# Two-layer graph attention on one core: both normalisations and one bound moved from VectorE to ScalarE, the centring term made by GpSimd, the mixed phase in another order

## Chip, cores, metric

One core of a Trainium2 chip. The metric is the device time of one launch in microseconds (us). The engines are named as in the profile: PE (TensorE matmul), PEld (its weight loads), DVE (VectorE), ACT (ScalarE), POOL (GpSimd), SP (SyncE, which issues the DMAs).

## What is computed

Sixteen graphs of 512 nodes and 256 channels pass two attention layers. Cut to what matters (biases left out):

```python
# layer 0: one head, masked by adj == 0
q, k = x @ Wq, x @ Wk
s = where(adj == 0, -1e18, q @ k.T / 16)
x = layernorm(x + (where(adj == 0, 0, softmax(s)) @ x) @ Wc)
# layer 1: 8 heads of 32 channels, weighted by the clipped adjacency
s = q_h @ k_h.T / sqrt(32) + log(clip(adj, 1e-8))
out = layernorm(x + concat_h(softmax(s) @ v_h) @ Wo)
```

A layer norm is (x - mean) / sqrt(var + 1e-5), then gamma and beta.

## The kernel before

**Phases.** All five engines run the same list of stages, each its own part of every stage, in the order of that list. `run` (line 422) goes through a first phase (front of graph 0), fifteen mixed phases (order `SCHEDULE`, line 73), a last phase (`LAST`) and an end. A mixed phase works on three graphs: the front of graph j (layer 0, then layer 1's q, k, v and the row maxima of head group 0), the back of graph i (row maxima of head group 1, scores, exponentials, masks and sums of layer 1), and the tail of graph t (output projection, second layer norm, store). `follow` (line 430) lets an engine skip stages in which it has no part; so where a stage stands in the list decides what stands in front of it on each engine's own queue.

**Stages of the front.** `split` makes a high and a low part of x transposed (ACT line 810, DVE line 948). `q0` projects (PE line 598, ACT 815, DVE 964). `bias` compares adj with zero (DVE line 977), which `max0` needs. `u` makes x @ Wc rows and one more column (ACT line 826). `max0` bounds each row's scores (PE lines 650 and 652, DVE line 989). `floor` adds a constant to that extra column (DVE line 995), `shift0` takes the smaller of the two bounds (DVE line 1000) and spreads it as a diagonal (ACT line 832), which the last steps of `scores0` add (PE lines 663 to 668); ACT takes the exponential (line 836). `context0` is the weighted sum (PE line 676), with four DVE instructions for each of four row tiles (1021 to 1029). `stats0` aggregates mean and variance (DVE 1036); POOL makes (var + eps) to the power -0.5 in two instructions (lines 1133, 1135); `norm0` is four DVE instructions, one for each row tile (line 1044). `transpose` turns them (PE 685, ACT 867, DVE 958), and `q1`, `k1`, `v` project (PE 598 and 620). `max1` is one matmul (line 698) and one maximum over 512 columns (DVE line 1005), sixteen in a group of heads; `mrow1` transposes the maxima (PE 703, DVE 1011), and a DMA puts them into the stack that `scores1` reads.

**Stages of the back and the tail.** `scores1` (quad, pair) is two matmuls (line 719), two exponentials (ACT 847) and one mask multiplication on POOL (line 1144), or on DVE where the list has a `mask` stage (line 985). `values1` and `denominators1` sum a quad (PE line 742). The exponentials of quad n wait for both sums of quad n-3. `sums_out` copies both accumulators out (ACT 856, 857), and `values1` and `denominators1` of quad 4 wait for it. `reciprocal` (four parts, DVE 1052), `normalise` (1057), `high_output` (ACT 862) and `low_output` (DVE 1061) prepare the projection `project` (PE 770, DVE 1070). `stats1`, `norm1` (four DVE instructions, line 1086) and `output` (two POOL instructions of 128x1024, lines 1156 and 1158) are the second layer norm; `residual` is two more POOL instructions of that size (1127, 1129), and `norm0` of the next graph waits for it.

**Banks.** Four PSUM banks (`misc`) go round through all stages of `MISC_DRAIN`, in the order of the list. A fill waits until the use four places before it has been read by its engine, so a late reader stops PE three uses on. `skip_front` and `skip_back` only count as a use.

**SP.** Its queue, in order: x transposed, half the stacks, a wait for `clip`, the next adjacency, the other stacks, the row of maxima of group 0 and the stacks of group 1, x, the store of the tail (waits for `output`), and the row of maxima of group 1.

## Time and profile before

| | |
|---|---|
| median of 3 runs | 1311.65 us (1310.07 to 1313.34) |
| the profiled execution's own time | 1313.88 us |
| its span | 1312.1 us |
| mean granted TensorE clock | 0.964 |
| PE busy | 1188.1 us, 91% |
| DVE busy | 1019.7 us, 78% |
| POOL busy | 733.7 us, 56% |
| ACT busy | 522.1 us, 40% |

All views below are of this one execution; times in them count from the start of its span. The first cast of a graph's transposed x (ACT line 810) marks the start of a phase: the first graph's starts at 18.4 us, the first mixed phase (which has no tail) at 86.4 us, the second at 158.6 us and the fifteenth at 1158.0 us, so that thirteen full mixed phases take 999.4 us, 76.9 us each. A line of a group gives the busy time, the mean of one instruction in ns, and the idle time of the engine just before them with what ended it. A granted clock of 1.00 is 2.4 GHz, of 0.50 it is 1.2 GHz.

### The profile page before, as it was taken

The page shows a single profiled execution, that of the slowest core. Times are in us where ns is not written, and L with a number is a line of the kernel's source. Part 1 is how long each engine was busy: PE and PEld are TensorE (multiplying, and loading weights), DVE is VectorE, ACT ScalarE, POOL GpSimd, SP SyncE. Part 2 cuts the span into 40 slices and gives each one's busy share as a digit, 9 for nine tenths or more (in the row PEclk, how much of TensorE's full clock was granted, in tenths as well). Part 3 has the DMA queues.
Part 4 walks back from the last instruction along what each step waited for, and adds up shares of the span by engine and source line. Part 5 has one row for each costly group of instructions (what it writes and reads, how often), then busy time and mean ns, then how long its engine had stood idle before and what let it go on. Part 6 is the DMA issues. An engine that isn't in the chain of part 4 may idle for free.

```text
span 1312.1 us, 21162 instructions
## 1 busy us (share of the span) xinstructions
PE 1188.1 (91%) x6474; PEld 697.3 (53%) x6474; DVE 1019.7 (78%) x1751; ACT 522.1 (40%) x1004; POOL 733.7 (56%) x352
## 2 busy tenths in 40 slices
PE   6889998989989898998989899998989989898883
PEld 5655464645546464554646456464655546465432
DVE  4365887978788787878879787887978788797874
ACT  2233444444344444434444443444444344444421
POOL 0016376483747648374774837467483746748362
PEclk8889999999999999999999999999999999999877
DMA  3041321404132140413214041321504132150310
GB/s 121 1 129 33 101 77 39 123 16 136 40 98 78 37 123 16 132 44 98 76 35 128 16 132 45 94 71 39 134 16 126 51 94 66 42 134 16 80 33 16
DMA packets 69652, 94.67 MB, mean 72 GB/s; under 512 B 14081, under 2 KB 32769, under 8 KB 69634
## 3 DMA queue, kind: packets, MB, share of 16 engines
q1 hardware_dynamic: 69634, 94.44, 25.7%
q8 instruction: 10, 0.16, 0.1%
q14 instruction: 8, 0.07, 0.0%
HBM read 35.40 MB, written 8.39 MB: 33 GB/s over the span
## 4 chain that ended last, share of the span: by engine, by line
PE 47%; POOL 20%; DVE 15%; issue 12%; ACT 4%; DVEq 1%; DMA 1%; POOLq 0%; ACTq 0%; SPq 0%
POOL PR L1144 10%; PE misc L598 9%; PE scores L719 6%; DVE mx L1005 5%; PE misc L698 5%; PE values L742 4%; PE denominators L742 4%; DVE xn L1044 4%; PE misc L608 3%; POOL z L1156 3%; PE misc L663 3%; PE misc L650 3%; POOL res L1127 2%; PE misc L620 2%; PE values L770 2%
## 5 line engine op out<-in xcount | busy, mean ns | idle before, releaser
L1144 POOL TENSOR_TENSOR PR<-PR,CLIP 128x1024 f32<-128x1024 f32 x217 | 529.6, 2458 | 453.9 <-ACT PR L847 453.9
L847 ACT ACTIVATE PR<-scores 128x512 f32<-128x512 f32 x512 | 278.5, 598 | 329.2 <-PE scores L719 321.3
L1005 DVE TENSOR_REDUCE mx<-misc 128x1 f32<-128x512 f32 x512 | 321.3, 680 | 52.6 <-PE misc L698 50.8
L719 PE MATMUL scores<-QS,KS 97*128 97x512 f32 x512 | 199.9, 469 | 8.6 <-issue 3.4
L742 PE MATMUL values<-PR,V 128*32 128x512 f32 x1024 | 135.6, 614 | 21.0 <-ACT sums_v L856 10.7
L719 PEld LDWEIGHTS scores<-QS,KS 97*128 97x128 f32 x512 | 89.9, 198 | 91.6 <-ACT PR L847 53.4
L698 PE MATMUL misc<-K1H,Q1H 32*128 32x512 f32 x512 | 128.0, 502 | 7.8 <-DVE K1L L964 4.0
L742 PE MATMUL denominators<-PR,ones 128*32 128x512 f32 x1024 | 134.2, 607 | 0.6 <-DVE z L1070 0.3
L1052 DVE RECIPROCAL sums_w<-sums_w 128x128 f32<-128x128 f32 x128 | 114.1, 925 | 10.0 <-issue 5.2
L676 PE MATMUL misc<-U,P 128*128 128x257 f32 x512 | 120.2, 383 | 0.0
L698 PEld LDWEIGHTS misc<-K1H,Q1H 32*128 32x128 f32 x512 | 54.9, 184 | 118.9 <-DVE mx L1005 50.0
L676 PEld LDWEIGHTS misc<-U,P 128*128 128x128 f32 x512 | 95.6, 189 | 17.7 <-issue 3.5
L1133 POOL TENSOR_TENSOR ve<-mv,eps 128x4 f32<-128x4 f32 x32 | 19.8, 617 | 104.7 <-DVE mv L1036 59.2
L836 ACT ACTIVATE P<-misc 128x512 f32<-128x512 f32 x64 | 38.3, 598 | 84.8 <-PE misc L668 84.8
L1044 DVE TENSOR_SCALAR xn<-X,mv,rstd 128x256 f32<-128x256 f32 x64 | 52.7, 887 | 19.4 <-POOL rstd L1135 19.4
L742 PEld LDWEIGHTS values<-PR,V 128*32 128x32 f32 x1024 | 23.7, 109 | 78.7 <-issue 37.1
L1086 DVE TENSOR_SCALAR z<-z,mv,rstd 128x256 f32<-128x256 f32 x64 | 51.9, 874 | 13.8 <-POOL rstd L1135 13.8
L1021 DVE TENSOR_SCALAR den<-misc 128x1 f32<-128x1 f32 x64 | 10.1, 158 | 67.3 <-PE misc L676 67.3
L663 PE MATMUL misc<-Q0H,XTH 128*128 128x512 f32 x128 | 57.6, 450 | 3.8 <-ACT P L836 3.8
L985 DVE TENSOR_TENSOR PR<-PR,CLIP 128x1024 f32<-128x1024 f32 x39 | 51.1, 1316 | 3.3 <-ACT PR L847 2.9
L989 DVE TENSOR_REDUCE mx<-misc 128x1 f32<-128x512 f32 x64 | 43.8, 685 | 9.7 <-PE misc L652 8.4
L663 PE MATMUL misc<-Q0L,XTH 128*128 128x512 f32 x128 | 50.9, 397 | 0.0
(159 smaller groups left out, 1996.4 us busy)
## 6 DMA issues: line engine op xcount, KB each, us to landing
ADJ<-adj_t SPq DMA_DIRECT2D x16, 1024.0 KB, 6.0
QS<-Q1H SPq DMA_DIRECT2D x256, 64.0 KB, 2.0
KS<-K1H SPq DMA_DIRECT2D x256, 64.0 KB, 2.0
P<-x_t SPq DMA_DIRECT2D x16, 512.0 KB, 3.8
X<-x SPq DMA_DIRECT2D x16, 512.0 KB, 3.7
QS<-Q1L SPq DMA_DIRECT2D x128, 64.0 KB, 2.0
KS<-K1L SPq DMA_DIRECT2D x128, 64.0 KB, 2.0
out<-z SPq DMA_DIRECT2D x16, 512.0 KB, 2.9
```

What stands on the lines that cost most here:

```text
L598: mm = pe.matmul(bank[:], w[:, k, P * c:P * (c + 1)], s[:, k, :], start=(n == 0), stop=(n == len(terms) - 1))
L663: pe.matmul(bank[:], kk[:, c, rows_k], qq[:, c, :], start=(n == 0), stop=False)
L676: mm = pe.matmul(bank[:, 0:D + 1], P0[:, k, P * t:P * (t + 1)], U[:, k, 0:D + 1], start=(k == 0), stop=(k == T - 1))
L698: pe.matmul(bank[:], Q1H[part, g, P * t:P * (t + 1)], K1H[part, g, :], start=True, stop=True).then_inc(misc_filled, 1)
L719: pe.matmul(ST[n][:], KS[:, h, P * k:P * (k + 1)], QS[:, h, :], start=True, stop=True).then_inc(scores_filled, 1)
L742: mm = pe.matmul(bank[DK * h:DK * (h + 1), :], w, PR[quad % WEIGHT_BUFFERS][:, h, :], start=(k == 0), stop=(k == T - 1))
L847: act.activation(PR[quad % WEIGHT_BUFFERS][:, h, :], ST[n][:], ACT.Exp, scale=SCALE1).then_inc(exp_done, 1)
L1005: dve.tensor_reduce(mx1[:, g, h, t:t + 1], misc_bank(ph, "max1", g, n)[:], AX.X, ALU.max, negate=True).then_inc(misc_drained["dve"], 1)
L1044: dve.tensor_scalar(xn[:, t, :], X[:, t, :], mv0[:, t, 0:1], rstd0[:, t:t + 1], ALU.subtract, ALU.mult).then_inc(xn_ready, 1)
L1052: dve.reciprocal(sums_w[:, q], sums_w[:, q]).then_inc(back_step, 1)
L1086: dve.tensor_scalar(z[:, t, :], z[:, t, :], mv1[:, t, 0:1], rstd1[:, t:t + 1], ALU.subtract, ALU.mult).then_inc(zn_ready, 1)
L1144: pool.tensor_tensor(w, w, clipped, ALU.mult).then_inc(masked_pool, 1)
```

## The change

- `norm0` and `norm1` leave DVE for ACT: one activation (Identity) for each row tile, with the scale rstd and the bias -mean * rstd, both read per partition.
- POOL makes that bias: `rstd` has four instructions in place of two.
- `floor` leaves DVE for ACT. `shift0` on DVE is a tensor_reduce (minimum) over the two bounds, which now lie side by side, in place of a tensor_tensor.
- `SCHEDULE` has the same 127 stages in another order. `FIRST` and `LAST` stay.

```diff
--- before.py
+++ after.py
@@ -71,28 +71,28 @@
 ]
 
 SCHEDULE = [
-    ("reciprocal", 1, 0), ("max1", 1, 0), ("split", 0), ("split", 1), ("reciprocal", 1, 1),
-    ("reciprocal", 1, 2), ("max1", 1, 1), ("q0", 0), ("q0", 1), ("bias",), ("scores1", 0, 0), ("u", 0),
-    ("scores1", 0, 1), ("u", 1), ("scores1", 1, 0), ("u", 2), ("reciprocal", 1, 3), ("max0", 0),
-    ("max0", 1), ("scores1", 1, 1), ("normalise", 1), ("max0", 2), ("u", 3), ("skip_back",), ("floor",),
-    ("low_output", 1), ("max1", 1, 2), ("max1", 1, 3), ("max1", 1, 4), ("high_output", 1), ("max0", 3),
-    ("project",), ("scores1", 2, 0), ("skip_back",), ("max1", 1, 5), ("shift0",), ("stats1",),
-    ("max1", 1, 6), ("values1", 0), ("values1", 1), ("denominators1", 0), ("norm1",), ("scores0", 0),
-    ("scores1", 2, 1), ("scores0", 1), ("scores0", 2), ("max1", 1, 7), ("max1", 1, 8), ("output",),
-    ("max1", 1, 9), ("scores0", 3), ("scores1", 3, 0), ("max1", 1, 10), ("max1", 1, 11), ("max1", 1, 12),
-    ("max1", 1, 13), ("denominators1", 2), ("denominators1", 1), ("values1", 2), ("max1", 1, 14),
-    ("max1", 1, 15), ("residual",), ("scores1", 3, 1), ("context0", 0), ("mrow1", 1), ("context0", 1),
-    ("context0", 2), ("scores1", 4, 0), ("mask", 4, 0), ("values1", 3), ("scores1", 4, 1), ("skip_back",),
-    ("context0", 3), ("skip_front",), ("scores1", 5, 0), ("denominators1", 3), ("sums_out", 0), ("stats0",),
-    ("mask", 5, 0), ("values1", 4), ("scores1", 5, 1), ("denominators1", 4), ("norm0",),
-    ("reciprocal", 0, 0), ("reciprocal", 0, 1), ("scores1", 6, 0), ("transpose", 0), ("scores1", 6, 1),
-    ("transpose", 1), ("reciprocal", 0, 2), ("reciprocal", 0, 3), ("values1", 5), ("scores1", 7, 0),
-    ("q1", 0), ("k1", 0), ("normalise", 0), ("q1", 1), ("max1", 0, 0), ("max1", 0, 1), ("max1", 0, 2),
-    ("denominators1", 5), ("max1", 0, 3), ("scores1", 7, 1), ("values1", 6), ("max1", 0, 4), ("max1", 0, 5),
-    ("max1", 0, 6), ("max1", 0, 7), ("denominators1", 6), ("clip",), ("k1", 1), ("denominators1", 7),
-    ("max1", 0, 8), ("max1", 0, 9), ("max1", 0, 10), ("high_output", 0), ("values1", 7), ("low_output", 0),
-    ("max1", 0, 11), ("max1", 0, 12), ("sums_out", 1), ("v", 0), ("max1", 0, 13), ("max1", 0, 14),
-    ("max1", 0, 15), ("v", 1), ("mrow1", 0),
+    ("split", 0), ("max1", 1, 0), ("split", 1), ("reciprocal", 1, 0), ("reciprocal", 1, 1),
+    ("reciprocal", 1, 2), ("q0", 0), ("q0", 1), ("bias",), ("skip_back",), ("u", 0), ("scores1", 0, 0),
+    ("max1", 1, 1), ("scores1", 0, 1), ("reciprocal", 1, 3), ("u", 1), ("scores1", 1, 0), ("max0", 0),
+    ("max0", 1), ("normalise", 1), ("u", 2), ("max0", 2), ("skip_back",), ("scores1", 1, 1),
+    ("low_output", 1), ("u", 3), ("floor",), ("max0", 3), ("max1", 1, 2), ("max1", 1, 3),
+    ("high_output", 1), ("max1", 1, 4), ("scores1", 2, 0), ("project",), ("max1", 1, 5), ("values1", 0),
+    ("values1", 1), ("shift0",), ("scores1", 2, 1), ("max1", 1, 6), ("max1", 1, 7), ("stats1",),
+    ("scores0", 0), ("scores0", 1), ("scores0", 2), ("norm1",), ("output",), ("scores0", 3), ("max1", 1, 8),
+    ("max1", 1, 9), ("max1", 1, 10), ("scores1", 3, 0), ("max1", 1, 11), ("max1", 1, 12),
+    ("denominators1", 0), ("max1", 1, 13), ("max1", 1, 14), ("max1", 1, 15), ("denominators1", 1),
+    ("values1", 2), ("scores1", 3, 1), ("context0", 0), ("residual",), ("mrow1", 1), ("context0", 1),
+    ("context0", 2), ("scores1", 4, 0), ("values1", 3), ("mask", 4, 0), ("skip_front",), ("scores1", 4, 1),
+    ("context0", 3), ("denominators1", 2), ("scores1", 5, 0), ("stats0",), ("denominators1", 3),
+    ("reciprocal", 0, 0), ("sums_out", 0), ("scores1", 5, 1), ("mask", 5, 0), ("norm0",),
+    ("denominators1", 4), ("scores1", 6, 0), ("values1", 4), ("transpose", 0), ("scores1", 6, 1),
+    ("reciprocal", 0, 1), ("skip_back",), ("transpose", 1), ("values1", 5), ("reciprocal", 0, 2),
+    ("reciprocal", 0, 3), ("scores1", 7, 0), ("q1", 0), ("k1", 0), ("scores1", 7, 1), ("q1", 1),
+    ("max1", 0, 0), ("max1", 0, 1), ("values1", 6), ("max1", 0, 2), ("max1", 0, 3), ("denominators1", 5),
+    ("max1", 0, 4), ("max1", 0, 5), ("max1", 0, 6), ("normalise", 0), ("denominators1", 6), ("clip",),
+    ("max1", 0, 7), ("high_output", 0), ("k1", 1), ("max1", 0, 8), ("max1", 0, 9), ("values1", 7),
+    ("denominators1", 7), ("max1", 0, 10), ("max1", 0, 11), ("max1", 0, 12), ("v", 0), ("low_output", 0),
+    ("sums_out", 1), ("max1", 0, 13), ("max1", 0, 14), ("max1", 0, 15), ("v", 1), ("mrow1", 0),
 ]
 
 LAST = [
@@ -260,6 +260,7 @@
         ones = sb("ones", [P, P])
         ones_r = sb("ones_r", [P, P], F32R)
         minus_half = sb("minus_half", [P, T])
+        minus_one = sb("minus_one", [P, T])
         eps = sb("eps", [P, T])
         scratch = sb("scratch", [P, 1])
 
@@ -283,8 +284,8 @@
         absent = sb("absent", [P, 1])
         Q0H, Q0L = (sb(n, [P, C, N], F32R) for n in ("Q0H", "Q0L"))
         U = sb("U", [P, T, 1 + D + 2])
-        mx0 = sb("mx0", [P, T])
-        floor0 = sb("floor0", [P, T])
+        bounds0 = sb("bounds0", [P, T, 2])
+        MAXIMUM, FLOOR = 0, 1
         nm0 = sb("nm0", [P, T])
         floor_bias = sb("floor_bias", [P, 1])
         NM0 = sb("NM0", [P, T, P], F32R)
@@ -296,6 +297,7 @@
         mv0 = sb("mv0", [P, T, 2])
         ve0 = sb("ve0", [P, T])
         rstd0 = sb("rstd0", [P, T])
+        centre0 = sb("centre0", [P, T])
         xn = sb("xn", [P, T, D])
         XNH, XNL = (sb(n, [P, C, N], F32R) for n in ("XNH", "XNL"))
         Q1H, Q1L, K1H, K1L = (sb(n, [P, C, N], F32R) for n in ("Q1H", "Q1L", "K1H", "K1L"))
@@ -325,6 +327,7 @@
         mv1 = sb("mv1", [P, T, 2])
         ve1 = sb("ve1", [P, T])
         rstd1 = sb("rstd1", [P, T])
+        centre1 = sb("centre1", [P, T])
 
         WQT, WKT, BQ_WIDE = res[:, 0:C, :], res[:, C:2 * C, :], xn[:, 0:C, 0:P]
         MISC = [ps(f"misc{n}", [P, N]) for n in range(MISC_BANKS)]
@@ -396,7 +399,7 @@
         out_stored = sem("out_stored")
 
         FIRST_LOADS, REST_LOADS = 3 + 1, 4 + 1
-        CONSTS = 9
+        CONSTS = 10
         block = ctx.enter_context(nc.Block())
 
         def misc_bank(ph, *stage):
@@ -825,6 +828,12 @@
                 wait_filled(act, ph, "u", t)
                 act.copy(U[:, t, 1:1 + D + 2], misc_bank(ph, "u", t)[:, 0:D + 2]).then_inc(misc_drained["act"], 1)
 
+            def floor(ph):
+
+                wait_drained(act, ph, "u", T - 1)
+                act.activation(bounds0[:, :, FLOOR], U[:, :, 1 + D], ACT.Identity,
+                               bias=floor_bias[:, 0:1]).then_inc(floor0_ready, 1)
+
             def shift0(ph):
 
                 act.wait_ge(nm0_ready, ph.j + 1)
@@ -866,10 +875,25 @@
                 wait_filled(act, ph, "transpose", c)
                 act.copy(XNH[:, c, :], misc_bank(ph, "transpose", c)[:]).then_inc(hi_written, 1)
 
+            def norm0(ph):
+                act.wait_ge(rstd0_ready, ph.j + 1)
+                if ph.back:
+
+                    act.wait_ge(res_ready, ph.i + 1)
+                for t in range(T):
+                    act.activation(xn[:, t, :], X[:, t, :], ACT.Identity, bias=centre0[:, t:t + 1],
+                                   scale=rstd0[:, t:t + 1]).then_inc(xn_ready, 1)
+
+            def norm1(ph):
+                act.wait_ge(rstd1_ready, ph.t + 1)
+                for t in range(T):
+                    act.activation(z[:, t, :], z[:, t, :], ACT.Identity, bias=centre1[:, t:t + 1],
+                                   scale=rstd1[:, t:t + 1]).then_inc(zn_ready, 1)
+
             do = {
-                "prepare": prepare, "split": split,
+                "prepare": prepare, "split": split, "norm0": norm0, "norm1": norm1,
                 "q0": lambda ph, c: hi(ph, "q0", c, Q0H, BQ0),
-                "u": context_rows, "shift0": shift0,
+                "u": context_rows, "floor": floor, "shift0": shift0,
                 "scores0": exp0, "transpose": xn_high,
                 "q1": lambda ph, c: hi(ph, "q1", c, Q1H, BQ1),
                 "k1": lambda ph, c: hi(ph, "k1", c, K1H, BK1),
@@ -890,6 +914,7 @@
             for part in Wc0:
                 dve.memset(part[:, :, D + 1:D + 2].bitcast(F32), 0.0).then_inc(consts_set, 1)
             dve.memset(minus_half[:], -0.5).then_inc(consts_set, 1)
+            dve.memset(minus_one[:], -1.0).then_inc(consts_set, 1)
             dve.memset(eps[:], LN_EPS).then_inc(consts_set, 1)
             dve.memset(U[:, :, 0:1], 1.0).then_inc(consts_set, 1)
             dve.memset(KS[MROW:STACK, :, :].bitcast(F32), 1.0).then_inc(consts_set, 1)
@@ -986,18 +1011,13 @@
 
             def max0(ph, t):
                 wait_filled(dve, ph, "max0", t)
-                dve.tensor_reduce(mx0[:, t:t + 1], misc_bank(ph, "max0", t)[:], AX.X,
+                dve.tensor_reduce(bounds0[:, t, MAXIMUM:MAXIMUM + 1], misc_bank(ph, "max0", t)[:], AX.X,
                                   ALU.max, negate=True).then_inc(misc_drained["dve"], 1)
-
-            def floor(ph):
-
-                wait_drained(dve, ph, "u", T - 1)
-                dve.tensor_scalar(floor0[:], U[:, :, 1 + D], floor_bias[:, 0:1], None, ALU.add).then_inc(floor0_ready, 1)
 
             def shift0(ph):
                 wait_drained(dve, ph, "max0", T - 1)
                 dve.wait_ge(floor0_ready, ph.j + 1)
-                dve.tensor_tensor(nm0[:], mx0[:], floor0[:], ALU.min).then_inc(nm0_ready, 1)
+                dve.tensor_reduce(nm0[:], bounds0[:], AX.X, ALU.min).then_inc(nm0_ready, 1)
 
             def max1(ph, g, n):
                 t, h = divmod(n, PER_GROUP)
@@ -1035,15 +1055,6 @@
                 for t in range(T):
                     dve.bn_aggr(mv0[:, t, :], st0[:, t, :]).then_inc(stats0_ready, 1)
 
-            def norm0(ph):
-                dve.wait_ge(rstd0_ready, ph.j + 1)
-                if ph.back:
-
-                    dve.wait_ge(res_ready, ph.i + 1)
-                for t in range(T):
-                    dve.tensor_scalar(xn[:, t, :], X[:, t, :], mv0[:, t, 0:1], rstd0[:, t:t + 1],
-                                      ALU.subtract, ALU.mult).then_inc(xn_ready, 1)
-
             def reciprocal(ph, g, part):
 
                 if part == 0:
@@ -1080,31 +1091,24 @@
                 for t in range(T):
                     dve.bn_aggr(mv1[:, t, :], st1[:, t, :]).then_inc(stats1_ready, 1)
 
-            def norm1(ph):
-                dve.wait_ge(rstd1_ready, ph.t + 1)
-                for t in range(T):
-                    dve.tensor_scalar(z[:, t, :], z[:, t, :], mv1[:, t, 0:1], rstd1[:, t:t + 1],
-                                      ALU.subtract, ALU.mult).then_inc(zn_ready, 1)
-
             do = {
                 "prepare": prepare, "split": split, "clip": clip, "bias": bias,
                 "q0": lambda ph, c: lo(ph, "q0", c, Q0L, Q0H, BQ0),
-                "mask": mask, "max0": max0, "floor": floor, "shift0": shift0, "context0": context0,
-                "stats0": stats0, "norm0": norm0, "stats1": stats1,
+                "mask": mask, "max0": max0, "shift0": shift0, "context0": context0,
+                "stats0": stats0, "stats1": stats1,
                 "transpose": xn_low,
                 "q1": lambda ph, c: lo(ph, "q1", c, Q1L, Q1H, BQ1),
                 "k1": lambda ph, c: lo(ph, "k1", c, K1L, K1H, BK1),
                 "max1": max1, "mrow1": mrow1, "reciprocal": reciprocal, "normalise": normalise, "low_output": low_output,
                 "project": add_residual,
-                "norm1": norm1,
             }
             run(dve, lambda ph: follow(ph, do))
 
 
         @block.gpsimd
         def _(pool):
-            POOL_STEPS0 = 1
-            POOL_STEPS1 = 2
+            POOL_STEPS0 = 3
+            POOL_STEPS1 = 4
 
             pool.memset(z[:, 0, 0:1], 0.0).then_inc(out_stored, 1)
             pool.memset(ident[:], 0.0).then_inc(ident_zeroed, 1)
@@ -1128,11 +1132,14 @@
                 pool.wait_ge(res_step, ph.i + 1)
                 pool.tensor_tensor(res[:], res[:], all_rows(S_RES), ALU.add).then_inc(res_ready, 1)
 
-            def rstd(var, ve, dst, step_sem, before, done):
-
-                pool.tensor_tensor(ve[:], var, eps[:], ALU.add).then_inc(step_sem, 1)
-                pool.wait_ge(step_sem, before + 1)
-                pool.tensor_tensor(dst[:], ve[:], minus_half[:], ALU.pow).then_inc(done, 1)
+            def rstd(moments, ve, dst, centre, step_sem, before, done):
+
+                pool.tensor_tensor(ve[:], moments[:, :, 1], eps[:], ALU.add).then_inc(step_sem, 1)
+                pool.tensor_tensor(centre[:], moments[:, :, 0], minus_one[:], ALU.mult).then_inc(step_sem, 1)
+                pool.wait_ge(step_sem, before + 2)
+                pool.tensor_tensor(dst[:], ve[:], minus_half[:], ALU.pow).then_inc(step_sem, 1)
+                pool.wait_ge(step_sem, before + 3)
+                pool.tensor_tensor(centre[:], centre[:], dst[:], ALU.mult).then_inc(done, 1)
 
             def mask(ph, quad, pair):
                 if (quad, pair) in dve_masks(ph.kind):
@@ -1145,16 +1152,16 @@
 
             def rstd0_of(ph):
                 pool.wait_ge(stats0_ready, ph.j * T + T)
-                rstd(mv0[:, :, 1], ve0, rstd0, pool_step0, ph.j * POOL_STEPS0, rstd0_ready)
+                rstd(mv0, ve0, rstd0, centre0, pool_step0, ph.j * POOL_STEPS0, rstd0_ready)
 
             def rstd1_of(ph):
                 pool.wait_ge(stats1_ready, ph.t * T + T)
-                rstd(mv1[:, :, 1], ve1, rstd1, pool_step1, ph.t * POOL_STEPS1, rstd1_ready)
+                rstd(mv1, ve1, rstd1, centre1, pool_step1, ph.t * POOL_STEPS1, rstd1_ready)
 
             def output(ph):
                 pool.wait_ge(zn_ready, ph.t * T + T)
                 pool.tensor_tensor(z[:], z[:], all_rows(S_G1), ALU.mult).then_inc(pool_step1, 1)
-                pool.wait_ge(pool_step1, ph.t * POOL_STEPS1 + 2)
+                pool.wait_ge(pool_step1, ph.t * POOL_STEPS1 + 4)
                 pool.tensor_tensor(z[:], z[:], all_rows(S_B1), ALU.add).then_inc(out_ready, 1)
 
             do = {"prepare": prepare, "residual": residual, "scores1": mask, "stats0": rstd0_of,
```

## Rows read from the trace of the kernel before

**Rows 1.** The page: busy time by engine, and the chain that ended last.

```profile
PE 1188.1 (91%) x6474; PEld 697.3 (53%) x6474; DVE 1019.7 (78%) x1751; ACT 522.1 (40%) x1004; POOL 733.7 (56%) x352
...
PE 47%; POOL 20%; DVE 15%; issue 12%; ACT 4%; DVEq 1%; DMA 1%; POOLq 0%; ACTq 0%; SPq 0%
```

**Rows 2.** Windows, two successive mixed phases: busy us (instructions), PEclk, DMA.

```profile
543.10:619.30 76.20, 71.27 (x402) 41.60 (x402) 62.68 (x108) 32.23 (x63) 46.94 (x22) 1.00 0.27 76
619.30:696.70 77.40, 72.52 (x402) 42.67 (x401) 62.78 (x108) 32.22 (x64) 46.89 (x22) 0.98 0.27 74
```

**Rows 3.** Who waited for whom, PE, one phase: total us, times, longest.

```profile
PE misc L685 <- DVE xn L1044: 1.7, 1, 1.7
PE values L742 <- POOL PR L1144: 0.7, 1, 0.7
PE values L742 <- ACT sums_v L856: 0.7, 1, 0.7
PE misc L598 <- DVE XTL L948: 0.5, 1, 0.5
...
PE misc L663 <- ACT P L836: 0.3, 1, 0.3
```

**Rows 4.** Groups by line, DVE, the same phase: busy, mean ns | idle before.

```profile
L1052 DVE RECIPROCAL sums_w<-sums_w 128x128 f32<-128x128 f32 x9 | 8.1, 928 | 0.7 <-issue 0.7
L1086 DVE TENSOR_SCALAR z<-z,mv,rstd 128x256 f32<-128x256 f32 x4 | 3.5, 940 | 0.8 <-POOL rstd L1135 0.8
L1044 DVE TENSOR_SCALAR xn<-X,mv,rstd 128x256 f32<-128x256 f32 x4 | 3.4, 920 | 1.2 <-POOL rstd L1135 1.2
...
L995 DVE TENSOR_SCALAR floor<-U,floor_bias 128x4 f32<-128x4 f32 x1 | 1.2, 1222 | 0.4 <-ACT U L826 0.4
```

**Rows 5.** Line 1000 over the whole run: ns min/median/max.

```profile
L1000 DVE TENSOR_TENSOR nm<-mx,floor x16: 162/2280/2287, 32.0 to 1177.2; 128x4 f32<-128x4 f32 x16
```

**Rows 6.** Groups by line, ACT, the phase after it.

```profile
L847 ACT ACTIVATE PR<-scores 128x512 f32<-128x512 f32 x32 | 17.4, 598 | 20.2 <-PE scores L719 20.2
...
L815 ACT ACTIVATE K1H<-misc,cols 128x512 fp32r<-128x512 f32 x2 | 1.4, 688 | 4.1 <-PE misc L598 4.1
...
L832 ACT ACTIVATE NM<-ident,nm 128x128 fp32r<-128x128 f32 x4 | 1.3, 391 | 2.5 <-DVE nm L1000 2.5
```

**Rows 7.** Timeline, POOL, the phase of group 3: start, us, [idle before].

```profile
571.35 2.39 POOL L1156 TENSOR_TENSOR z<-z,spread 128x1024 f32<-128x1024 f32 x1 [0.55 <-DVE z L1086]
...
583.22 2.36 POOL L1144 TENSOR_TENSOR PR<-PR,CLIP 128x1024 f32<-128x1024 f32 x1
...
590.97 1.09 POOL L1133 TENSOR_TENSOR ve<-mv,eps 128x4 f32<-128x4 f32 x1 [0.26 <-DVE mv L1036]
592.13 1.02 POOL L1135 TENSOR_TENSOR rstd<-ve,minus_half 128x4 f32<-128x4 f32 x1
```

**Rows 8.** Timeline, ACT, the same phase.

```profile
570.95 0.60 ACT L836 ACTIVATE P<-misc 128x512 f32<-128x512 f32 x1 [1.26 <-PE misc L668]
...
590.61 0.59 ACT L856 COPY sums_v<-values 128x512 f32<-128x512 f32 x1 [0.16 <-PE denominators L742]
...
598.47 0.60 ACT L867 CAST XNH<-misc 128x512 fp32r<-128x512 f32 x1
```

**Rows 9.** Timeline, DVE, the same phase.

```profile
590.80 1.19 DVE L985 TENSOR_TENSOR PR<-PR,CLIP 128x1024 f32<-128x1024 f32 x1
593.19 3.42 DVE L1044 TENSOR_SCALAR xn<-X,mv,rstd 128x256 f32<-128x256 f32 x4 [1.19 <-POOL rstd L1135]
...
599.11 0.69 DVE L958 TENSOR_TENSOR XNL<-misc,XNH 128x512 fp32r<-128x512 f32 x1 [0.29 <-ACT XNH L867]
...
604.42 0.68 DVE L1057 TENSOR_TENSOR sums_v<-sums_v,sums_w 128x512 f32<-128x512 f32 x1
```

**Rows 10.** Timeline, PE, the same phase.

```profile
592.25 0.73 PE L719 MATMUL scores<-QS,KS 97*128 97x512 f32 x2
```

**Rows 11.** Timeline, DVE, the end.

```profile
1302.49 1.38 DVE L1086 TENSOR_SCALAR z<-z,mv,rstd 128x256 f32<-128x256 f32 x4 [1.41 <-POOL rstd L1135]
```

## Prediction

> **What bounds the kernel now.** I read the page first. PE is busy for 91% of the span, DVE for 78%, POOL for 56%, ACT for 40%, and the chain that ended last lies on PE for 47%, on POOL for 20% and on DVE for 15% [rows 1]. So PE is near its bound, and what can be won is the time in which it waits. The windows show how regular the work is: one mixed phase takes 76.2 us at a granted clock of 1.00, the next 77.4 us at 0.98, since a stretch of it ran at 1.2 GHz [rows 2]. The mean over thirteen phases is 76.9 us, so that lower clock costs about 0.7 us a phase. The waits of PE in the undisturbed phase are the third view: 1.7 us for the normalised rows xn, 0.7 for a mask of POOL, 0.7 for ACT's copy of the sums, 0.5 for the low part of x, 0.3 for an exponential [rows 3]. They make 3.9 us of 76.2: the whole stake of the steady part is 15 x 3.9 = 58 us, and moving work off DVE pays only where DVE ends one of these waits.
>
> **What leaves DVE.** In a phase norm1 costs it 3.5 us, norm0 3.4, floor 1.2 [rows 4] and shift0's tensor_tensor 2.3 [rows 5]. One of the four norm instructions and shift0 are long because POOL holds something that they need: line 1000 takes 162 ns at its shortest and 2280 at the median [rows 5]. As a tensor_reduce it costs between these two; I take 0.16, since the only other tensor_reduces here, with PSUM operands, are never long. That is an inference across memories, so 2.28 stays as the other end. The Trainium skill (VectorE: DVE Perf Modes, "Two Vector instructions with no wait between them") has only instructions with two SBUF tensor inputs, or in a two-port mode, use the read interface that is shared with GpSimd; by it the tensor_reduce is free of POOL, and no row shows one on SBUF. Together DVE loses 3.5 + 3.4 + 1.2 + 2.1 = 10.2 us of 76. Nearly all of it is cover, not path: I cost it at nothing but in the parts below, as PE's waits for DVE are xn and the low part of x alone.
>
> **What it costs ACT.** No row has a scale and a bias from memory at once. An activation of 512 columns takes 598 ns with neither and 688 with a bias, so one operand is 90 ns; 128 columns with a scale take 391 [rows 6]. 256 columns with one operand lie between, 391 + (688 - 391)/3 = 490, and the second operand makes 580. Bounds: 391 and 688. Successive ones overlap by about 90, so a norm is 0.58 + 3 x 0.49 = 2.05 us (1.3 to 2.5), against 3.42 on DVE now in a mixed phase [rows 9] and 1.38 where POOL is idle [rows 11]. The Trainium skill prices a ScalarE instruction with SBUF source at 224 cycles of 1.2 GHz plus the columns (VectorE: DVE Perf Modes, "The TRN2 errata"): 400 ns for 256 columns, and 293 for the 128 of the row that took 391. With 400 a norm would be about 1.3 us and each wait behind it 0.7 shorter. The row contradicts it, so the measurement decides.
>
> **What it costs POOL.** Two more instructions of 128x4 in each rstd. Their like takes 0.20 us free and 1.09 while DVE runs a mask beside it (590.97 against DVE's 590.80) [rows 7, 9]; with handovers I take 0.55 us for both, between 0.5 and 2.2.
>
> **The sum for a mixed phase, part by part.**
> (a) The low part of x (wait 0.5) comes earlier: DVE now has a reciprocal (0.93, [rows 4]) and a maximum ahead of both splits, then only a maximum between them. But three reciprocals in place of two then stand ahead of `bias`, which max0 needs. I take +0.3 (0 to 0.5).
> (b) values1 of quad 3 waits 0.7 for POOL [rows 3]. POOL now does output (two of 2.4), mask (3,0), residual (two of 2.35) and only then mask (3,1). In the new list residual is behind mask (3,1): 4.7 us less ahead of it, against output starting later, since ACT runs norm1 only behind the third exponential of layer 0. From that exponential's end it takes 2.05 + 2 x 2.4 + 2 x 2.4 = 11.7 us until mask (3,1) is done. Now it is done at 585.58 [rows 7], 14.0 us after the exponential's end at 571.55 [rows 8], and PE has by then waited 0.7; in the new order PE has nearly the same work in between, so over 13 us. +0.7 (0 to 0.9). SP's store waits for output in front of the second row of maxima; output still ends before mrow1 (1), so nothing there.
> (c) The fourth exponential of layer 0 now stands behind norm1 on ACT. It comes ready 1.86 us after the third one's start (0.60 and 1.26 idle, [rows 8]); ACT is free after 0.60 + 2.05 = 2.65, so it is 0.8 later, and its bank is needed three uses on, by max1 (1, 11). The present 0.3 goes, 0.8 comes: -0.5 (0 to -1.0).
> (d) The chain to q1. Now it takes from the copy of the sums at 590.61 [rows 8] to the end of the second low part at 599.80 [rows 9], 9.2 us, with 3.42 of norm0 in it. In the new order ACT is full from that copy on: copies 1.1, exponentials (5,1) 1.1, norm0 2.05, exponentials (6,0) 1.1, high part 0.6, exponentials (6,1) 1.1, high part 0.6, then DVE's 0.7: 8.3 us. +0.9 (-0.3 to +1.3, the ends by POOL's price above and ACT's). It holds only if rstd and its bias are there when ACT has done (5,1), about 2.2 us after the copies begin. Cover gone, each us of lateness is a us of path.
> (e) The end of the phase. Behind the second Q1 part DVE runs sixteen maxima without rest. One scores1 pair (0.73 for two that overlap what follows, [rows 10], so 0.55) now stands ahead of q1 (1), and normalise (0.68, [rows 9]) falls into that run: -1.2. The copy of v and the casts of the next x follow v1 on ACT, and v1 no longer ends last: +0.6. Together -0.6 (0 to -1.2).
> (f) The clock: a shorter wait at the split may save some of the 0.7; I take +0.2 (-0.7 to +0.7).
> Sum: 0.3 + 0.7 - 0.5 + 0.9 - 0.6 + 0.2 = 1.0 us a phase, 15 us over fifteen.
>
> **Outside the mixed phases** the old orders stay and POOL is idle, so the move costs: 0.55 on POOL and 2.05 - 1.38 on ACT, 1.2 us, once in the first phase ahead of the transposes and once at the end, ahead of the last output [rows 11]. In the last phase norm1 stands between exponentials that wait for PE anyway; nothing. -2.4 us.
>
> In all 12.6 us. The profiled execution's own time is 1313.9, 2.2 above the median; 1313.9 - 12.6 = 1301.3, and against the median 1311.65 - 12.6 = 1299.
>
> **Rivals.** About 0.3% (4 us) is what a measurement of this kernel can tell from no change.
> Slower, by one mechanism: the fourth POOL instruction of rstd0 meets DVE's mask (5,0). The new list puts that mask right behind a reciprocal which starts when the sums are out, so it asks for SBUF while POOL is in its power (1.02, [rows 7]); DVE goes first, the bias comes 1.2 us late as ve does now [rows 7, 9], ACT waits, and with it exponentials and transposes. It decides if the mask starts before POOL's fourth begins. Then (d) is -0.3, a phase loses 0.2: 3 + 2.4 = 5.4 us, 1317. If PE's longer rest there also brings a stretch at 1.2 GHz into every phase (1.2 us in the seven or so that have none), it is 1325. For it: the times of my sum put the two within 0.2 us. Against: ACT's own queue gives 0.5 us of play. 0.25.
> The tensor_reduce waits for POOL as the tensor_tensor does, so that the change of form does not do what it is for: the diagonal comes 2.1 us later, and of this two sums, a scores pair and six matmuls of scores0 cover all but 0.4: 1299 + 6 = 1305. In the range of the forecast.
> The waits only move: PE's work is the same, more and shorter runs of max1 (fifteen for twelve) and more changes between kinds of matmul give most of it back: three runs at 0.2 to 0.3 us each leave 0.2 us of the 1.0, so 3 - 2.4, a gain below 1 us: 1311, no change that can be told. 0.15.
> Better: (c) and (e) cost nothing and the clock never falls: 1.0 + 0.5 + 0.6 = 2.1 us a phase, 31 - 2.4 = 29 us, 1283. 0.08.
>
> **Numbers.** The forecast, 1299, has 0.52 and runs from 1288 to 1308. Faster by over 0.3%: 0.49 of it and the 0.08, 0.57. Within 0.3%: 0.03 and 0.15, 0.18. Slower: 0.25. The range takes in the collision at 1317 but not all of the 1325: 1284 to 1319.
>
> **What would show it.** Right: a mixed phase of about 75.9 us; no wait of PE for POOL's mask; line 1044's wait gone and xn made in 2.0 us; tensor_reduce at 0.16; PE's wait for an exponential of layer 0 up to 0.8. Wrong: norm instructions of ACT far from 0.58, POOL's last rstd instruction at 1 us or more, a phase above 76.9, the granted clock below 0.964.

## The result, and the profile after

The changed kernel takes 1325.3 us (median of 4 runs, 1323.46 to 1326.39) against 1312.49 in the same session: a ratio of 1.0097, 95% interval 1.0074 to 1.012. It is slower by 12.8 us where 12.6 us less were forecast, and outside the range. The profiled execution took 1323.46 us (span 1321.6; before 1313.88 and 1312.1).

The page of the changed kernel: busy time by engine, the chain that ended last, the costliest line whose mean is not what it was.

```profile
PE 1209.8 (92%) x6458; PEld 702.2 (53%) x6474; DVE 919.2 (70%) x1608; ACT 590.0 (45%) x1148; POOL 752.9 (57%) x416
...
PE 54%; DVE 20%; ACT 12%; issue 10%; POOL 1%; DMA 1%; DVEq 1%; ACTq 0%; POOLq 0%; SPq 0%
...
L1072 DVE TENSOR_TENSOR OTL<-sums_v,OTH 128x512 fp32r<-128x512 f32 x32 | 51.9, 1623 | 26.1 <-ACT OTH L871 26.1
```

DVE lost 100 us of busy time [rows 1], POOL left the chain, and PE is busy 22 us longer for the same matmuls. Line 1072, the low part of layer 1's output (`low_output`), took 22.9 us in all before, a mean of 716 ns. It now takes 51.9. Its source view (ns min/median/max, and who waited):

```profile
L1072 DVE TENSOR_TENSOR OTL<-sums_v,OTH x32: 684/693/2766, 156.6 to 1301.4; 128x512 fp32r<-128x512 f32 x32
...
  PE values L773: 24.2, 14
```

PE waits for it fourteen times, once in each mixed phase that has a tail, 1.7 us each; no such wait is in [rows 3]. Windows, two successive mixed phases of the changed kernel, and the stretch of `project` in the second:

```profile
468.90:545.40 76.50, 72.53 (x401) 41.67 (x400) 56.14 (x98) 36.49 (x72) 48.17 (x26) 1.00 0.27 76
545.40:623.10 77.70, 73.96 (x400) 43.08 (x400) 56.23 (x98) 36.49 (x73) 48.16 (x26) 0.98 0.27 75
```
```profile
558.90:566.00 7.10, 5.38 (x32) 4.74 (x30) 5.73 (x6) 1.90 (x5) 5.83 (x3) 0.79 0.56 146
```

Of thirteen phases eight take 77.6 to 77.7 us, five 76.5; the mean is 77.2 (before 76.9). The long ones run at 1.2 GHz for a while right behind the wait (the 0.79 above is the mean of the stretch), and that costs 1.2 us each. PE's waits in the second of them:

```profile
PE values L773 <- DVE OTL L1072: 1.7, 1, 1.7
PE denominators L745 <- ACT sums_w L866: 0.5, 1, 0.5
...
PE misc L601 <- DVE XTL L973: 0.2, 1, 0.2
```

The waits for xn (1.7) and for POOL's mask (0.7) of [rows 3] are gone, as forecast; one of 1.7 us, which no part of the sum had, has come. Timelines of ACT, DVE and POOL where it arises:

```profile
558.93 0.30 ACT L834 ACTIVATE bounds<-U,floor_bias 128x4 f32<-128x4 f32 x1
559.14 0.60 ACT L871 CAST OTH<-sums_v 128x512 fp32r<-128x512 f32 x1
...
559.78 2.73 DVE L1072 TENSOR_TENSOR OTL<-sums_v,OTH 128x512 fp32r<-128x512 f32 x1 [1.77 <-ACT OTH L871]
...
556.81 5.15 POOL L1151 TENSOR_TENSOR PR<-PR,CLIP 128x1024 f32<-128x1024 f32 x2
```

POOL's last row is two masks; the second of them starts at 559.60. The low part needs 0.68 us when nothing holds it. It is issued at 559.78, when that mask has run for 0.18 us, and ends 0.55 us behind it. In the kernel before, `floor` stood on DVE directly ahead of it, and the next mask came in just behind (timeline of before, DVE; the mask there starts at 557.55 and takes 2.91):

```profile
556.40 1.22 DVE L995 TENSOR_SCALAR floor<-U,floor_bias 128x4 f32<-128x4 f32 x1 [0.45 <-ACT U L826]
557.53 0.68 DVE L1061 TENSOR_TENSOR OTL<-sums_v,OTH 128x512 fp32r<-128x512 f32 x1
```

The moved pieces themselves came out as priced. Timelines of ACT, DVE and POOL of the changed kernel: norm1, shift0, the four instructions of rstd0 and the mask (5,0) beside them.

```profile
576.26 2.07 ACT L890 ACTIVATE z<-z,centre,rstd 128x256 f32<-128x256 f32 x4
...
567.85 0.15 DVE L1020 TENSOR_REDUCE nm<-bounds 128x4 f32<-128x8 f32 x1
...
596.34 1.02 POOL L1140 TENSOR_TENSOR rstd<-ve,minus_half 128x4 f32<-128x4 f32 x1
597.43 0.20 POOL L1142 TENSOR_TENSOR centre<-centre,rstd 128x4 f32<-128x4 f32 x1
...
597.88 1.16 DVE L1010 TENSOR_TENSOR PR<-PR,CLIP 128x1024 f32<-128x1024 f32 x1
```

The mixed phases are not the whole loss against before. Of the 9.5 us between the two profiled spans, the thirteen full mixed phases have 4.2, the time ahead of the first mixed phase 1.6, and the stretch from the start of the fifteenth to the end 4.4 (158.5 us where before it was 154.1); the first mixed phase is 0.7 us shorter. In the last phase PE stands longer ahead of scores1 (4,0), 6.1 us by its row where before it was 3.4. Timelines of ACT, POOL, SP's queue and PE:

```profile
1261.77 1.08 ACT L856 ACTIVATE PR<-scores 128x512 f32<-128x512 f32 x2 [7.41 <-PE values L745]
1262.73 2.07 ACT L890 ACTIVATE z<-z,centre,rstd 128x256 f32<-128x256 f32 x4
...
1267.31 3.24 POOL L1165 TENSOR_TENSOR z<-z,spread 128x1024 f32<-128x1024 f32 x1
...
1270.58 0.40 SPq L474 DMA_DIRECT2D out<-z  x1
1271.02 0.52 SPq L454 DMA_DIRECT2D QS<-nm  x1
...
1273.81 1.19 PE L722 MATMUL scores<-QS,KS 97*128 97x512 f32 x2 [6.14 <-issue]
```

norm1 waits on ACT behind an exponential, POOL's output ends later, SP's store waits for that output, and the row of maxima that PE needs is issued behind the store.

### The profile page after: what moved, and what is told of

Its sections match the earlier page's. It is cut to its first block, busy times and chain, and to the rows that moved or that the text cites. A ratio compares the mean times of both kernels' runs of the same rounds, so it can differ in the third digit from the quotient of the medians.

```text
span 1321.6 us, 21225 instructions
## 1 busy us (share of the span) xinstructions
PE 1209.8 (92%) x6458; PEld 702.2 (53%) x6474; DVE 919.2 (70%) x1608; ACT 590.0 (45%) x1148; POOL 752.9 (57%) x416
## 4 chain that ended last, share of the span: by engine, by line
PE 54%; DVE 20%; ACT 12%; issue 10%; POOL 1%; DMA 1%; DVEq 1%; ACTq 0%; POOLq 0%; SPq 0%
PE misc L679 9%; PE misc L601 6%; DVE mx L1025 6%; PE misc L666 6%; PE scores L722 5%; PE denominators L745 5%; PE values L745 5%; PE misc L623 4%; DVE sums_w L1063 4%; DVE OTL L1072 3%; PE misc L701 3%; ACT PR L856 3%; PE denominators L773 3%; ACT z L890 2%; ACT xn L884 2%
## 5 line engine op out<-in xcount | busy, mean ns | idle before, releaser
L1151 POOL TENSOR_TENSOR PR<-PR,CLIP 128x1024 f32<-128x1024 f32 x217 | 551.3, 2565 | 422.7 <-ACT PR L856 422.6
L1025 DVE TENSOR_REDUCE mx<-misc 128x1 f32<-128x512 f32 x512 | 320.3, 684 | 113.4 <-PE misc L701 113.0
L701 PE MATMUL misc<-K1H,Q1H 32*128 32x512 f32 x512 | 142.8, 504 | 8.5 <-ACT P L845 2.6
L1010 DVE TENSOR_TENSOR PR<-PR,CLIP 128x1024 f32<-128x1024 f32 x39 | 74.9, 1923 | 6.8 <-ACT PR L856 6.5
L1072 DVE TENSOR_TENSOR OTL<-sums_v,OTH 128x512 fp32r<-128x512 f32 x32 | 51.9, 1623 | 26.1 <-ACT OTH L871 26.1
L1163 POOL TENSOR_TENSOR z<-z,spread 128x1024 f32<-128x1024 f32 x16 | 37.7, 2356 | 55.2 <-ACT z L890 55.2
L871 ACT CAST OTH<-sums_v 128x512 fp32r<-128x512 f32 x32 | 19.6, 614 | 92.1 <-DVE sums_v L1068 92.1
L841 ACT ACTIVATE NM<-ident,nm 128x128 fp32r<-128x128 f32 x64 | 20.5, 390 | 90.1 <-DVE nm L1020 90.1
L823 ACT COPY V<-misc 128x512 f32<-128x512 f32 x32 | 18.7, 586 | 74.8 <-PE misc L623 74.8
L1137 POOL TENSOR_TENSOR ve<-mv,eps 128x4 f32<-128x4 f32 x32 | 6.5, 202 | 79.1 <-DVE mv L1056 57.1
```

Of the source, the lines that this page charges most:

```text
L701: pe.matmul(bank[:], Q1H[part, g, P * t:P * (t + 1)], K1H[part, g, :], start=True, stop=True).then_inc(misc_filled, 1)
L1010: dve.tensor_tensor(w, w, clipped, ALU.mult).then_inc(masked_dve, 1)
L1025: dve.tensor_reduce(mx1[:, g, h, t:t + 1], misc_bank(ph, "max1", g, n)[:], AX.X, ALU.max, negate=True).then_inc(misc_drained["dve"], 1)
L1072: dve.tensor_tensor(OTL[:, g, :], sums_v[:], OTH[:, g, :].bitcast(F32), ALU.subtract).then_inc(output_low, 1)
L1151: pool.tensor_tensor(w, w, clipped, ALU.mult).then_inc(masked_pool, 1)
```

## The experiments

The theories named in the expectations: **P**, the low part of the output loses a boundary between two of POOL's masks; **O**, the new order costs; **E**, ACT's new work costs. Each run gives its ratio to the kernel before with a 95% interval.

**The order alone.** Engines as before:

```diff
-SCHEDULE = [ the order before ]
+SCHEDULE = [ the new order ]
```

> The new order alone, all instructions on the engines of before. Theory O (the loss comes from the order: in it high_output (1) is queued on ACT behind u (3) and low_output (1) asks for SBUF in the middle of a mask of POOL, so project waits): slower than the changed kernel, since DVE now also carries the 10 us of norms and bounds, 1335 to 1360, and PE waits for the low part (the instruction in front of project) 1.5 us or more in each phase. Theory E (the loss comes from the engines: longer chains through ACT and POOL): at most 1315, with no such wait.

1432.9 us, 1.0916 (1.0898 to 1.0934), a phase 85.3 us: far worse than either theory gave. Who waited for whom, PE, one phase:

```profile
PE misc L685 <- DVE xn L1044: 3.7, 2, 2.0
PE values L742 <- DVE z L1070: 2.1, 1, 2.1
```

The new order needs the new engines: norm0 and `floor`, both on DVE here, each meet a mask (the first two instructions of norm0 take 2.44 and 2.42 us, `floor` 2.36). Not the low part, though; it is issued at 600.77, 0.14 us before the next mask starts, and takes 0.73.

**The engines alone.** The changed kernel in the order of before.

> The old order with the new engines. Theory O: faster than before by what xn and the diagonal gain, less 1.2 in the first phase, 1.2 at the end and some 3 in the last phase: 1290 to 1308, and the low part of quad group 1 takes 0.68 us as before. Theory E: 1320 or more, xn's wait on PE longer than 1.7.

1329.3 us, 1.0121 (1.0104 to 1.0138): the time that theory E gave, but not its mechanism, a wait for xn above 1.7 us. PE's waits, one phase, and timelines of ACT and POOL:

```profile
PE values L745 <- POOL PR L1151: 1.9, 1, 1.9
...
PE misc L688 <- ACT xn L884: 0.3, 2, 0.2
```
```profile
575.25 2.08 ACT L890 ACTIVATE z<-z,centre,rstd 128x256 f32<-128x256 f32 x4 [2.53 <-POOL centre L1142]
...
578.85 2.38 POOL L1151 TENSOR_TENSOR PR<-PR,CLIP 128x1024 f32<-128x1024 f32 x1 [3.63 <-ACT PR L856]
```

xn's wait falls from 1.7 to 0.3, as the engines were meant to bring, but the wait for POOL grows from 0.7 to 1.9. The low part takes 0.88 us here: `floor` stands in front of the cast on ACT as in the changed kernel, but in this order the low part is still issued 0.29 us before the next mask starts. So order and engines are each slower alone, by different waits, and only together do they give the wait of the changed kernel.

**norm1 back on DVE in the old order.** The kernel just shown with `norm1` as before:

```diff
-act.activation(z[:, t, :], z[:, t, :], ACT.Identity, bias=centre1[:, t:t + 1], scale=rstd1[:, t:t + 1])
+dve.tensor_scalar(z[:, t, :], z[:, t, :], mv1[:, t, 0:1], rstd1[:, t:t + 1], ALU.subtract, ALU.mult)
```

> The old order with the new engines (1329.3 us), but norm1 back on DVE. If its loss was that norm1 stands behind the third exponential of layer 0 on ACT, so that POOL's output and with it mask (3,1) come late: PE's wait for POOL before values1 of quad 3 goes back from 1.9 to 0.7 us or less, a phase to about 75 to 76 us, and the kernel to 1290 to 1300 us. If the loss was elsewhere (a fuller ACT, the clock): 1320 to 1329 us, with that wait still above 1.5.

1287.9 us, 0.9803 (0.9776 to 0.9829), a little below the range given; ten of thirteen phases take 74.7 to 74.8 us, and no wait for POOL is left. So in the old order the move of norm1 alone costs 41 us. The reason is not the one that the expectation gives, for in this order norm1 stands ahead of layer 0's exponentials. By the two rows of the kernel above, ACT stands idle for 2.53 us until POOL has made the bias, then runs norm1, and only then the first exponential of layer 0 and those of scores1 (2,1). POOL waits 3.63 us for these before it can mask them, and its output and mask (3,1) come behind that.

**The form of shift0 alone.** The kernel before with

```diff
-dve.tensor_tensor(nm0[:], mx0[:], floor0[:], ALU.min)
+dve.tensor_reduce(nm0[:], bounds0[:], AX.X, ALU.min)
```

> Before, with nothing changed but shift0 as a tensor_reduce over two bounds side by side (floor still on DVE, as a tensor_scalar). If a tensor_reduce on SBUF needs nothing of POOL it takes 0.15 us and DVE is 2.1 us ahead there; PE waited little for the diagonal, so 0 to 0.7 us a phase: 1300 to 1312. If its gain in the changed kernel came from another alignment, it takes up to 2.3 us here too.

1295.5 us, 0.9862 (0.9844 to 0.9881), faster than was expected; eleven of thirteen phases take 75.2 to 75.3 us. Timelines of DVE and POOL, and PE's first wait:

```profile
558.80 0.15 DVE L1000 TENSOR_REDUCE nm<-bounds 128x4 f32<-128x8 f32 x1
...
558.70 2.38 POOL L1144 TENSOR_TENSOR PR<-PR,CLIP 128x1024 f32<-128x1024 f32 x1 [1.75 <-ACT PR L847]
```
```profile
PE misc L685 <- DVE xn L1044: 1.7, 1, 1.7
```

One instruction, 2.28 to 0.15 us, brings 18 us. It is issued 0.10 us after a mask of POOL has begun and does not wait for it. norm1 then starts 1.9 us earlier in its phase and, no longer held up by a mask, ends 4.0 us earlier; POOL's output starts 0.8 us earlier, and PE's wait for the mask is gone. Only two of thirteen phases still have a stretch at 1.2 GHz; before, seven had one.

**The cast ahead.** The changed kernel with the cast of layer 1's output earlier on ACT:

```diff
-    ("u", 2), ("max0", 2), ...
+    ("u", 2), ("high_output", 1), ("max0", 2), ...
-    ("high_output", 1), ("max1", 1, 4), ("scores1", 2, 0), ("project",)
+    ("max1", 1, 4), ("scores1", 2, 0), ("project",)
```

> The changed kernel with high_output (1) moved in the order from behind u (3) and floor to behind u (2), so that DVE's low part can start about 1.8 us earlier and misses or meets an earlier mask of POOL. Theory O: the wait of project (1.7 us as PE shows it, 3.4 us of stage time) falls by 1 us or more a phase: 1300 to 1312. Theory E: no change, 1322 to 1328.

1286.2 us, 0.979 (0.9772 to 0.9809), better than theory O gave; a phase 74.4 us, `project` 3.0 us. Timeline of DVE:

```profile
545.29 2.11 DVE L1072 TENSOR_TENSOR OTL<-sums_v,OTH 128x512 fp32r<-128x512 f32 x1
```

It is issued in the middle of a mask (544.00 to 546.85) and takes 2.11 us, but ends before PE needs it.

**`floor` behind the cast.** A smaller cut: two ACT instructions change places, 0.30 us of work.

```diff
-    ("u", 3), ("floor",), ("max0", 3), ("max1", 1, 2), ("max1", 1, 3), ("high_output", 1),
+    ("u", 3), ("max0", 3), ("max1", 1, 2), ("max1", 1, 3), ("high_output", 1), ("floor",),
```

> The changed kernel with floor (one ACT instruction of 0.30 us) moved from in front of high_output (1) to behind it, nothing else. Theory P (the low part asks for SBUF 0.18 us after a mask of POOL has begun and so waits for the whole mask): 0.26 us earlier it gets in ahead of that mask, ends 2 us earlier, and project waits 2 us less in each phase: 1293 to 1303. Theory Q (it is the queue on ACT that counts, and POOL's mask only adds a delay of its own each time): 0.26 us a phase, 1320 to 1323.

1282.5 us, 0.9766 (0.9751 to 0.9781), again better than expected. Timelines of ACT and DVE, the window of one phase, PE's waits in it:

```profile
547.31 0.64 ACT L871 CAST OTH<-sums_v 128x512 fp32r<-128x512 f32 x1
547.83 0.32 ACT L834 ACTIVATE bounds<-U,floor_bias 128x4 f32<-128x4 f32 x1
...
547.98 0.76 DVE L1072 TENSOR_TENSOR OTL<-sums_v,OTH 128x512 fp32r<-128x512 f32 x1 [1.44 <-ACT OTH L871]
```
```profile
533.90:608.10 74.20, 72.18 (x401) 41.55 (x400) 54.19 (x98) 36.35 (x72) 48.20 (x26) 1.00 0.29 79
```
```profile
PE denominators L745 <- ACT sums_w L866: 0.5, 1, 0.5
PE misc L706 <- DVE mx L1025: 0.4, 2, 0.2
PE misc L653 <- DVE ABSENT L1002: 0.2, 1, 0.2
PE misc L701 <- issue: 0.2, 1, 0.2
PE misc L601 <- DVE XTL L973: 0.2, 1, 0.2
PE misc L701 <- ACT P L845: 0.2, 1, 0.2
```

All thirteen full phases take 74.2 us, none with a stretch at 1.2 GHz: 43 us for 0.3 us of ACT's time a phase. The low part is issued 0.2 us before the running mask ends, is through at 548.74, and the next mask waits for it (2.85 us).

**0.3 us of nothing in front.** The kernel just shown, with one idle instruction on ACT in the old place of `floor`:

```diff
+                if g == 1 and ph.kind == "steady":
+                    act.activation(idle[:], minus_half[:], ACT.Identity, bias=floor_bias[:, 0:1])
                 act.copy(OTH[:, g, :], sums_v[:]).then_inc(output_high, 1)
```

> The kernel with floor behind the cast (1282.5 us), and in the full mixed phases one more ACT instruction ahead of the cast of layer 1's output: 128x4, reading constants alone, written where nobody reads. It does about 0.3 us of nothing in the place where the changed kernel has floor. Theory P (the low part of the output loses the boundary between two masks of POOL by a tenth or two, and nothing else is at stake): the low part asks about 0.3 us later, behind the start of the mask, takes 2.4 to 2.8 us instead of 0.76, project takes 6.4 us instead of 3.0, a phase about 77.2 us, and the kernel 1318 to 1327 us. Theory Q (it mattered that the bound was kept out of the way of the layer-0 work, or that floor's result came later): it stays at 1280 to 1286 us, 0.3 us a phase at most.

1319.3 us, 1.0065 (1.0038 to 1.0092), phases of 76.5 and of 77.6 to 77.7 us. Timelines of ACT and DVE, and PE's first wait:

```profile
558.04 0.32 ACT L872 ACTIVATE idle<-minus_half,floor_bias 128x4 f32<-128x4 f32 x1
558.24 0.62 ACT L874 CAST OTH<-sums_v 128x512 fp32r<-128x512 f32 x1
...
558.90 2.90 DVE L1075 TENSOR_TENSOR OTL<-sums_v,OTH 128x512 fp32r<-128x512 f32 x1 [1.63 <-ACT OTH L874]
```
```profile
PE values L774 <- DVE OTL L1075: 1.7, 1, 1.7
```

The mask starts at 558.88, the low part 0.02 us later, and that is enough (in the kernel before it started 0.02 us earlier than the mask, and was not held). P holds: work that computes nothing brings the loss back, and outside `project` and the stage behind it the matmuls of a phase follow each other as without it, to 0.04 us a stage. One detail was off: `project` takes 5.0 us in a phase at full clock (5.8 to 6.5 where 1.2 GHz follows).

**norm0 back on DVE**, from the kernel with the cast ahead, with the edit shown for norm1.

> The kernel with the cast ahead of max0 2 (1286.2 us, 74.4 us a phase), but norm0 back on DVE. By step (d) of the prediction norm0 on ACT made the chain to q1 shorter by 0.9 us a phase, so this one has xn's wait back (1 to 1.7 us for PE) and 75.3 to 75.8 us a phase, 1298 to 1306 us. If the chain was covered anyway (as norm1's engine was of no account): 1282 to 1288 us.

1364.1 us, 1.0389 (1.0364 to 1.0414): a phase is 5.2 us longer, not 0.9, and the time is far above either range. Timeline of DVE (the first of four), and PE's wait:

```profile
613.66 1.16 DVE L1001 TENSOR_TENSOR PR<-PR,CLIP 128x1024 f32<-128x1024 f32 x1
614.74 2.44 DVE L1055 TENSOR_SCALAR xn<-X,mv,rstd 128x256 f32<-128x256 f32 x1
```
```profile
PE misc L688 <- DVE xn L1055: 3.7, 2, 2.0
```

DVE's own mask (5,0) goes first, and by then a mask of POOL runs, from 613.83 on. The first of the four is done 0.16 us behind that mask, the second, issued 0.11 us after the next mask has begun, waits in the same way for that one (2.43 us), the other two take 0.40: 5.43 us for norm0 against 2.07 on ACT.

**norm1 back on DVE**, from the same kernel.

> The early cast, with norm1 back on DVE (POOL still makes four instructions). Theory: the fourth exponential of layer 0 is no longer late, but norm1 on DVE meets POOL's masks and takes up to 3.5 us of DVE in a stretch where DVE has slack; DVE is not short there: 1283 to 1292, and the last phase gets about 2.8 us back. Rival (it is the relief of DVE that makes the order good): over 1295.

1279.8 us, 0.9754 (0.9739 to 0.9769): a phase takes 74.4 to 74.5 us either way, and it is 6.4 us less in all. In the profiled executions the stretch from the start of the fifteenth mixed phase to the end falls from 156.1 to 150.5 us; the wait before scores1 (4,0) has 2.3 of this (6.13 to 3.81 us). In the new order the move of norm1 brings nothing in a mixed phase and costs something at the end.

**shift0 as a tensor_tensor**, from the same kernel.

> The early cast, with shift0 as a tensor_tensor over the two bounds again. Theory P: DVE asks for it while the mask of POOL that the low part delayed is running, so it takes up to 2.3 us in place of 0.15; of these 2.1 the sums, a scores pair and six matmuls cover most: 0 to 0.7 us a phase, 1286 to 1297. Rival (the form is of no account in this order): 1285 to 1288 with a duration near 0.15.

1284.4 us, 0.9785 (0.9764 to 0.9807), no difference. Its source view:

```profile
L1020 DVE TENSOR_TENSOR nm<-bounds x16: 151/197/2075, 34.0 to 1147.7; 128x4 f32<-128x4 f32 x16
```

The 2075 ns are those of the first mixed phase. In the later ones it is issued at the very end of a mask (at 552.25, where the mask runs to 552.39) and has almost nothing to wait for. What was worth 18 us in the old order is worth nothing here.

**The row of maxima first.** The same kernel, in the last phase on SP:

```diff
-            store(B - 2)
             load_second_mrow(last)
+            store(B - 2)
```

> The kernel with the early cast, and on SP in the last phase the row of maxima of group 1 goes ahead of the store of the tail. Theory: in the changed kernel PE stands 6.1 us in the last phase before scores1 (4, 0), since that row waits behind the store, which waits for output, which waits for norm1 on ACT; before it was 3.4. With the row first it is about 2.5: 3 to 4 us less than with the early cast alone, 1281 to 1284. Rival (the wait is for something else, the stacks or the maxima themselves): 1285 to 1288.

1280.3 us, 0.975 (0.9736 to 0.9763), 5.9 us less, where the wait before scores1 (4,0) is 3.3 shorter (6.13 to 2.80). Timeline of PE, and the windows of the 13 us that follow the wait, with the cast ahead alone and here:

```profile
1236.64 1.19 PE L722 MATMUL scores<-QS,KS 97*128 97x512 f32 x2 [2.80 <-issue]
```
```profile
1236.35:1249.35 13.00, 12.48 (x42) 3.63 (x42) 6.60 (x6) 6.41 (x12) 4.74 (x3) 0.51 0.01 1
...
1236.64:1249.64 13.00, 12.34 (x52) 3.79 (x52) 10.69 (x7) 7.06 (x14) 9.68 (x4) 0.65 0.12 42
```

The stretch from the start of the fifteenth mixed phase to the end falls from 156.1 to 150.2 us, so all of the gain lies there: 3.3 is the wait, and 2.4 comes behind it. With the long wait PE runs at 1.2 GHz for 12.8 us behind it, with the short one for 9.2 (8.8 with norm1 on DVE). By my estimate from these figures the 3.6 us less at half the clock are worth 1.8 of the 2.4.

**All that helped.** `floor` behind the cast, the row first, norm1 on DVE.

> What helped, together: floor behind the cast (1282.5 us by itself), in the last phase the row of maxima ahead of the store on SP (its wait 6.4 to 3.1 us), and norm1 on DVE (its share 0 in a full phase). If they add up: 1282.5 - 3 to 6 = 1276 to 1280 us. If norm1 on DVE moves the low part of the output again behind the start of a mask: above 1300 us, with project at over 4 us.

1275.5 us (1273.6 to 1278.18, 5 runs), 0.9714 (0.9692 to 0.9735): the fastest, 2.9% below the kernel before and 3.8% below the changed one, and just under what was expected if the three add up; a phase is 74.2 us.

Its wait before scores1 (4,0) is 3.8 us, no shorter than with norm1 on DVE alone: those two do not add up. With norm1 on DVE the store is issued before the row is ready and no longer holds it. DVE does, for its mask in front of the row takes 2.20 us in place of 1.22, and the row is issued (at 1229.92) as soon as DVE has written it.

## Why the prediction was wrong

**The step that failed** is the term for `floor` on ACT, and with it the path that goes through it. "What it costs ACT" prices the norms alone, and "What leaves DVE" puts the rest at nothing ("Nearly all of it is cover, not path: I cost it at nothing"). It counted what DVE no longer does and did not follow `floor` to where it went. On ACT it stands in front of the cast, so the low part of the output is issued 0.3 us later, and in the new order that is behind the start of a mask. No part of the sum has the low part, the cast or `project`. The operation is of the class whose price the prediction did give for shift0 and norm0, a DVE instruction that POOL holds up: [rows 5] with 162 and 2280 ns. [rows 3] has no wait for it, and its mean of 716 ns looked harmless; but in the kernel before its mask began 0.02 us behind it. Cost: 77.2 against 74.2 us over thirteen phases, 39 us, and 2.7 us in the fifteenth mixed phase.

**Without it the forecast was too low a gain**: with `floor` behind the cast a phase is 74.2 us, 2.7 below the 76.9 of before, where the sum gave 1.0. By its parts, as PE's waits show them:

- (a) +0.3: right, XTL 0.5 to 0.2.
- (b) +0.7: right, the wait for POOL is gone.
- (c) -0.5: wrong sign but small, the exponential's wait is 0.2 against 0.3.
- (d) +0.9: too small. All 1.7 of xn's wait is gone, and in this order norm0 on DVE would cost 5.2 more, not 0.9; its length on ACT, 2.05, was right to 0.03, and rstd was there in time.
- (e) -0.6: not seen; the waits for XNL and XTH (0.4 and 0.3 before) are not in the list, which ends at 0.2, and only the copy of the sums has 0.5.
- (f) +0.2: too small; the shorter waits brought back all of the 0.7, every full phase is at 1.00.

The waits shown fall from 4.8 to 1.7 us and the phase at full clock from 76.2 to 74.2: about 1.1 us of 3.1 was given back between stages (PE's busy time rises from 71.3 to 72.2), which the rival "the waits only move" had right in kind.

**Two readings were off.** The prediction says that PE's waits for DVE are xn and the low part of x alone, and that all waits make 3.9 us. The list of [rows 3] goes on behind its gap; it makes 4.8, and has two more of DVE's, this one and one of 0.2:

```profile
PE misc L598 <- DVE XNL L958: 0.4, 1, 0.4
```

And DVE's busy time fell by 6.6 us a phase (62.7 to 56.1), not 10.2: the low part takes 2.0 more, and DVE's own mask (4,0), now issued while POOL's residual runs, 3.0 instead of 1.2.

**Relief of DVE at nothing** is wrong in the old order: the tensor_reduce alone brings 18 us, since shift0 stood ahead of norm1, and norm1 ahead of POOL's output. The path ran over DVE, then POOL, and PE's wait for POOL was its end. The 0.16 was right.

**"In the last phase norm1 stands between exponentials that wait for PE anyway; nothing"**: 2.8 us, through POOL and a store ahead of the row of maxima on SP. The end cost what was forecast: from the last statistics to POOL's output it is 4.0 us where before it was 2.9, 1.1 for the 1.2.

**The slower rival** gave 1317 and with a stretch at 1.2 GHz 1325, the time that came, but not by its mechanism, so that the match is luck: the fourth POOL instruction of rstd0 takes 0.20 us and is over 0.25 us before the mask (5,0) starts. What it had right is the kind: an instruction that finds POOL and DVE in each other's way, and 1.2 GHz behind PE's wait. Its 0.25 was on the wrong pair of instructions.

**What stays open**: why 1.2 GHz follows the 1.7 us wait in eight phases and not in the other five; why the first phase is 65 to 72 us long in the profiled executions of these kernels.
